# Two selective-scan layers on one core: D·u summed by TensorE, y gated straight out of PSUM, softplus sums and a Newton step on GpSimd, more scan inputs turned

## The chip, the cores and the metric

One Trainium2 chip, of which one core runs the whole program in one launch. The metric is the device time of one execution in microseconds; lower is better.

## What is computed

Four layers over x, float32, of shape (4, 128, 64, 64): a sparse 4096×4096 attention with a convolution (layer 0), a selective state-space scan with a depthwise convolution beside it (layer 1), a rank-one attention (layer 2), and a two-way selective scan with a group norm (layer 3). Only layers 1 and 3 are touched. Their core is the same:

```python
delta = softplus(dt @ W_dtr + b_dtr)                 # one rate per channel and step
h_l   = exp(delta_l * A) * h_(l-1) + delta_l * B_l * u_l   # N states per channel
y_l   = sum_n h_l[:, n] * C_l[n] + u_l * D
# layer 1: 128 channels, N = 64, one direction, 4 x 4096 steps; out = x + (y + conv) @ W_out
# layer 3: 256 channels, N = 16, 16384 steps forward, then 16384 backward;
#          out_dir = (y * silu(z)) @ W_out; the sum of both goes to the group norm
```

In layer 1, u is a layer-normed projection, so each step needs rsqrt(var), made from a root by logarithm and exponential and one Newton step.

## The kernel before, in words

Both scan layers work on 128 channels (partitions) and 1024 steps at a time. Layer 1 has 16 such **chunks** (index K), each with 64 states: 64 scans. Layer 3 has 64 **visits** (index S: 32 blocks of steps times two channel halves e, where K = S // 2; the first 32 visits run forward in time, the last 32 backward), each with 16 scans. States are handled in pairs P, k or r being the pair's number in its chunk (32 pairs) or visit (8 pairs). All order is written out by hand: each engine has its own list of steps, and semaphores join them. For every pair:

- ScalarE (ACT) writes the two decays exp(delta·A) of 128×1024 (`decays`, L884 and L1818). The second state of a pair, the odd one, has its channel halves swapped: it reads `crossed`, which two DMAs copy from `delta` once a chunk (`cross_delta`), after the last decay of the chunk before in layer 1.
- The input delta·B·u of the even state is made in one of two ways. *Broadcast*: TensorE (PE) spreads a row of B over 128 partitions into PSUM (`broadcast_B`, L702 and L1596) and VectorE (DVE) multiplies it by `du` in place (`even_input`, L1115 and L2005). *Turned*: ACT scales the transposed `duT` by B in eight 128×128 pieces (`turned_input`, L900; `odd_input` in layer 3, L1831) and PE transposes them back into PSUM (`turn_back`, L716 and L1606). The odd state's input is always turned; in layer 1, for the pairs in MADE, GpSimd (POOL) does the scaling instead, in one instruction (`odd_input`, L1025).
- DVE scans the two states (`scan`, L1128 and L2022), with the decay from SBUF and the input from PSUM. It may be at most four scans ahead of POOL's products (HS = 4), and ACT at most four decays ahead of DVE's scans (DS = 4).
- POOL multiplies h by the row C, which a DMA has broadcast into the same buffer (`product`, L1014 and L1943).
- PE adds the products up over the states in PSUM (`add_pair`, L733 and L1623), two pairs later. It uses the four 64×64 tiles of the array, own half to own half and own half to other half. Each float32 product appears as two instructions, so that a phase of `add_pair` is eight and a pair has two phases.

Once a chunk or visit comes the rest: projections and convolution on PE, softplus on ACT and POOL (`delta_copy`, `soft_exp`, `soft_log`, `soft_low`, `soft_max`, `soft_sum`, `input_rate`), u·D + y by DVE out of PSUM (`add_y`), then a POOL pass that adds the convolution (`add_conv`, L1008) or multiplies by the gate (`gating`, L1936). In layer 1 `rstds` and `newton` (L1069 to L1079) run on DVE at k = 7, and PE's `prep_rstd` and DVE's `scale_u` follow. In layer 3 `soft_max` (L1981) is on DVE at r = 3. PE keeps to its list: a step of it that waits holds up the `turn_back` and `broadcast_B` behind it, for which DVE's scans wait.

## Time and profile before

| | us |
|---|---|
| median of 3 runs (lowest, highest) | 10184.17 (10183.94, 10192.5) |
| profiled execution, its own time | 10189.69 |
| its span, first to last instruction | 10187.9 |
| busy in the span: PE, DVE, ACT, POOL | 9232.4, 8216.2, 7986.1, 5614.9 |
| layer 1: first scan to last scan | about 2840 to 5720 |
| layer 3: first scan to last scan | about 6784 to 10098 |

Layers 0 and 2 and the ends take the rest. An engine's busy share over the whole span mixes four layers and says little. What is needed is a table for stretches inside layer 1, the forward half of layer 3 and its backward half, divided by the number of chunks or visits that went by, which the number of scans gives. In a timeline row the columns are start, busy time, engine, line and operation, and the last bracket is the idle time before it and what ended that. Instructions overlap a little at their ends, so the price of one in a full queue is the distance between starts.

### The profile page before, as it was taken

The numbers are of one execution on the slowest core, as the hardware profiler recorded it, in microseconds if no ns is written. First come the engines' busy times: TensorE is split into PE (matmuls) and PEld (weight loads), VectorE is DVE, ScalarE is ACT, GpSimd is POOL, SyncE is SP. The second block draws the span as 40 slices with busy tenths as digits, with TensorE's granted clock in tenths as the row PEclk, the third lists the DMA queues.
The fourth block names the chain that finished last, engine by engine and source line by source line (L and its number), as shares of the span: only waits on it lengthen the run. The fifth ranks groups of instructions, "written<-read, shape, count | busy, mean of one in ns | idle before, by whom it ended". The sixth has DMA issues, their size and how long they took to land. (4 is left out here: it accounts for less than half of the span.)

```text
span 10187.9 us, 146443 instructions
## 1 busy us (share of the span) xinstructions
PE 9232.4 (91%) x51396; PEld 4770.3 (47%) x51396; DVE 8216.2 (81%) x6150; ACT 7986.1 (78%) x14637; POOL 5614.9 (55%) x2852
## 2 busy tenths in 40 slices
PE   9999999999988888888888999988899998888885
PEld 6767767767633333333433444433333333333332
DVE  7858858768589999999999511149999999999997
ACT  5646646646488999999999655569999999999995
POOL 0000000000089999999999300038888888888885
PEclk9999999999989999999999999999999999999997
DMA  0000000000055655555555200025555656556566
GB/s 39 0 1 0 0 1 0 0 0 0 3 170 190 191 189 186 196 191 193 188 193 196 84 8 8 8 91 193 195 199 193 199 195 201 192 194 201 193 197 225
DMA packets 338542, 1249.78 MB, mean 123 GB/s; under 512 B 39280, under 2 KB 39408, under 8 KB 334448
## 3 DMA queue, kind: packets, MB, share of 16 engines
q1 hardware_dynamic: 338032, 1243.13, 36.9%
q8 instruction: 301, 4.93, 0.2%
q14 instruction: 209, 1.71, 0.0%
HBM read 1144.41 MB, written 56.62 MB: 118 GB/s over the span
## 5 line engine op out<-in xcount | busy, mean ns | idle before, releaser
L1943 POOL TENSOR_TENSOR l_ring<-l_h,l_ring 128x1024 f32<-128x1024 f32 x1024 | 2095.1, 2058 | 517.7 <-DVE l_h L2022 516.3
L2022 DVE TENSOR_TENSOR_SCAN l_h<-l_ring,l_h,l_ps 128x1024 f32<-128x1024 f32 x960 | 2200.0, 2333 | 13.7 <-PE l_ps L1606 0.7
L1014 POOL TENSOR_TENSOR l_hc<-l_h,l_hc 128x1024 f32<-128x1024 f32 x1024 | 2027.9, 2000 | 165.4 <-DVE l_h L1128 144.2
L1128 DVE TENSOR_TENSOR_SCAN l_h<-l_decay,l_h,l_ps 128x1024 f32<-128x1024 f32 x768 | 1746.8, 2329 | 11.8 <-PE l_ps L716 5.0
L116 POOL COPY l_qm<-l_q 128x128 f32 x128 | 82.8, 648 | 2577.4 <-PE l_ps L188 2181.1
L900 ACT ACTIVATE l_xt<-l_duT,l_BT 128x128 f32<-128x128 f32 x4096 | 1247.3, 389 | 40.7 <-PE l_ps L716 40.2
L1831 ACT ACTIVATE l_xt<-l_duT,l_BT 128x128 f32<-128x128 f32 x4096 | 1246.8, 389 | 0.0
L1623 PE MATMUL l_ps<-l_ring,w_sb 64*64 64x512 f32 x8192 | 1170.1, 642 | 1.0 <-PE l_ps L1623 0.4
L733 PE MATMUL l_ps<-l_hc,w_sb 64*64 64x512 f32 x8192 | 1134.3, 624 | 0.6 <-PE l_ps L733 0.4
L212 PE MATMUL l_ps<-l_attnT,l_vT 128*128 128x128 f32 x8192 | 1096.5, 277 | 1.3 <-ACT l_attnT L283 1.3
L212 PEld LDWEIGHTS l_ps<-l_attnT,l_vT 128*128 128x128 f32 x8192 | 1014.8, 192 | 138.0 <-issue 114.7
L188 PE MATMUL l_ps<-l_k,l_qm 128*128 128x512 f32 x2048 | 1055.4, 600 | 16.7 <-DVE l_E L395 16.7
L716 PEld LDWEIGHTS l_ps<-w_sb,l_xt 128*128 128x128 f32 x5888 | 641.1, 142 | 878.2 <-DVE l_h L1128 714.0
L716 PE MATMUL l_ps<-w_sb,l_xt 128*128 128x128 f32 x5888 | 824.5, 283 | 231.0 <-DVE l_h L1128 154.9
L1255 PE MATMUL l_ps<-l_E,l_hs 128*128 128x512 f32 x2048 | 880.0, 592 | 5.2 <-DVE l_hs L1321 5.2
L401 DVE SCALAR_TENSOR_TENSOR l_E<-l_relu,l_E 128x1024 f32<-128x1024 f32 x512 | 626.6, 1224 | 287.3 <-ACT l_E L276 287.3
L276 ACT ACTIVATE l_E<-l_E,l_offsets 128x1024 f32<-128x1024 f32 x512 | 587.0, 1146 | 290.8 <-DVE l_E L395 290.7
L270 ACT ACTIVATE l_relu<-l_ps,l_offsets 128x1024 f32<-128x1024 f32 x512 | 570.8, 1115 | 273.6 <-PE l_ps L188 271.9
L1282 ACT ACTIVATE l_E<-l_g,l_neg_max,l_f 128x4096 f32<-128x4096 f32 x128 | 486.4, 3800 | 379.4 <-PE l_ps L1255 367.5
L1606 PEld LDWEIGHTS l_ps<-w_sb,l_xt 128*128 128x128 f32 x4096 | 477.5, 149 | 648.3 <-DVE l_h L2022 588.6
L1606 PE MATMUL l_ps<-w_sb,l_xt 128*128 128x128 f32 x4096 | 605.2, 295 | 172.6 <-DVE l_h L2022 170.4
L201 PEld LDWEIGHTS l_ps<-w_sb,l_E 128*128 128x128 f32 x4096 | 507.3, 141 | 410.2 <-issue 393.1
(238 smaller groups left out, 15173.8 us busy)
## 6 DMA issues: line engine op xcount, KB each, us to landing
l_hc<-l_rows_dram SPq DMA_DIRECT2D x1024, 512.0 KB, 4.7
l_ring<-l_rows_dram SPq DMA_DIRECT2D x1024, 512.0 KB, 4.9
l_crossed<-l_delta SPq DMA_DIRECT2D x160, 256.0 KB, 3.8
l_gate_dram<-l_gate SPq DMA_DIRECT2D x32, 512.0 KB, 6.6
l_recon_dram<-l_recon SPq DMA_DIRECT2D x32, 512.0 KB, 6.4
l_gate<-l_gate_dram SPq DMA_DIRECT2D x32, 512.0 KB, 5.5
l_xw<-x_dram SPq DMA_DIRECT2D x30, 513.5 KB, 6.2
x_dram<-x SPq DMA_DIRECT2D x16, 512.0 KB, 2.6
```

What stands on the lines that cost most here:

```text
L188: ins = nc.tensor.matmul(logits[c % 2][:, j * BANK:(j + 1) * BANK], qm[:, h, :], k[:, c * CH + j * BANK:c * CH + (j + 1) * BANK], start=Tr ...
L212: ins = nc.tensor.matmul(ps[:, bank, 0:128], vT[:, t * 128:(t + 1) * 128], attnT[:, g % 2, j * 128:(j + 1) * 128], start=t == 0, stop=t == ...
L716: ins = nc.tensor.transpose(state_bank(odd, hf)[:, t * 128:(t + 1) * 128], xt[:, (n + hf) % XS, t * 128:(t + 1) * 128], ident)
L733: ins = nc.tensor.matmul(ps[to, 4 + j, :], ident[own, own], hc[own, (2 * P + odd) % CS, half(j)], start=k == 0 and phase == 0, stop=k == P ...
L900: ins = nc.scalar.activation(into, own if odd else own[:, ::-1, :], ACT.Identity, scale=BT[:, p, blk, at:at + 1])
L1014: nc.gpsimd.tensor_tensor(hc[:, unit % CS, :], h[:, unit % HS, window(unit)][:, along(K)], hc[:, unit % CS, :], ALU.mult).then_inc(hc_done, 1)
L1128: nc.vector.tensor_tensor_scan(h[:, unit % HS, window(unit)][:, along(K)], decay[:, unit % DS, :], odd_in if odd else even_in, before, ALU ...
L1606: ins = nc.tensor.transpose(odd_bank(hf)[:, t * 128:(t + 1) * 128], xt[:, (2 * P + hf) % XS, t * 128:(t + 1) * 128], ident)
L1623: ins = nc.tensor.matmul(ps[to, 4 + j, :], ident[own, own], hc[own, (2 * P + odd) % CS, half(j)], start=r == 0 and phase == 0, stop=r == P ...
L1831: ins = nc.scalar.activation(xt[:, (2 * P + hf) % XS, t * 128:(t + 1) * 128], duT[:, S % 2, 4 * hf + t, :], ACT.Identity, scale=BT[:, K % ...
L1943: nc.gpsimd.tensor_tensor(hc[:, unit % CS, :], h[:, unit % HS, window(unit)][:, along], hc[:, unit % CS, :], ALU.mult).then_inc(hc_done, 1)
L2022: nc.vector.tensor_tensor_scan(h[:, unit % HS, window(unit)][:, into], decay[:, unit % DS, order], x_now[:, order], before, ALU.mult, ALU. ...
```

## The change

What it does, in both scan layers:

1. u·D is no longer computed by DVE. The weights hold D as a diagonal matrix, and PE adds D·u to the sum of states in PSUM, in the two own-half tiles, once a chunk or visit, in `add_pair` of pair 4.
2. DVE's one pass over the sum now adds the convolution (layer 1) or multiplies by the gate (layer 3) directly; POOL's passes `add_conv` and `gating` go. In layer 1 `gate_conv` moves from k = 1 to k = 0, ahead of it.
3. Softplus: ACT makes |z| and relu(z) from PSUM in halves; the full-width Abs, its drain and layer 1's full-width Relu go. In layer 3 `soft_max` becomes a plain addition on POOL.
4. Layer 1's Newton step moves to POOL (k = 7, ahead of the products); squares, variance and roots come one or two pairs earlier.
5. Layer 1 turns 16 even states a chunk instead of 14, and POOL makes 15 odd inputs instead of 14, in another pattern. Layer 3, which turned no even state and had POOL make none, now turns one a visit forward and two backward, and POOL makes two odd inputs a visit.
6. `delta` and `z1` start two elements further in; in layer 3 the rows of B and C sit at partitions 0 to 31 of `rest`, so POOL's `split_rest` waits for the turned B and for the stored rows.

The diff, cut to its core:

```diff
-TURNED = (1, 2, 3, 5, 7, 8, 9, 11, 15, 18, 25, 26, 29, 31)
-MADE = (0, 1, 3, 5, 8, 9, 13, 14, 15, 18, 19, 21, 29, 31)
+TURNED = (1, 2, 3, 5, 7, 9, 10, 11, 14, 18, 23, 25, 26, 28, 29, 31)
+MADE = (0, 1, 3, 5, 7, 10, 11, 13, 17, 19, 21, 23, 28, 29, 31)
...
+        delta = sb("delta", [128, 2, CH + 4])[:, :, 2:CH + 2]
+        z1, z2 = sb("z1", [128, CH + 4])[:, 2:CH + 2], sb("z2", [128, CH])
...
                 for own, other, j in ((lower, upper, phase), (upper, lower, 1 - phase)):
+                    if k == 4:
+                        nc.tensor.matmul(ps[own, 4 + j, :], wt("D")[own, own], u[own, P // PAIRS % 2, half(j)],
+                                         start=False, stop=False)
...
-                        if k in (2, 3):
-                            prep_u(K + 1, k - 2)
-                        if k == 7:
+                        if k in (1, 2):
+                            prep_u(K + 1, k - 1)
+                        if k == 5:
...
             def delta_copy(K, p, j):
                 act.wait_ge(delta_mm, 2 * K + j + 1)
-                nc.scalar.activation(delta[:, p, half(j)], prep_ps, ACT.Identity,
+                if j == 0:
+                    act.wait_ge(rows_stored, 16 * K + 16)
+                nc.scalar.activation(z1[:, half(j)], prep_ps, ACT.Abs, bias=wt("dtr_b"))
+                nc.scalar.activation(delta[:, p, half(j)], prep_ps, ACT.Relu,
                 act.wait_ge(delta_out, 2 * K + 2)
-                act.wait_ge(rows_stored, 16 * K + 16)
-                nc.scalar.activation(z1[:], delta[:, p, :], ACT.Abs)
-                act.drain()
                 nc.scalar.activation(z1[:], z1[:], ACT.Exp, scale=-1.0).then_inc(exp_ln, 1)
-                nc.scalar.activation(delta[:, p, :], delta[:, p, :], ACT.Relu)
...
-                        if k == 7:
+                        if k == 6:
...
+            def newton(K):
+                pool.wait_ge(root_ready, K + 1)
+                nc.gpsimd.tensor_tensor(tmp[:], var[:], root[:], ALU.mult)
+                pool.drain()
+                nc.gpsimd.tensor_tensor(tmp[:], tmp[:], root[:], ALU.mult)
+                pool.drain()
+                nc.gpsimd.tensor_scalar(tmp[:], tmp[:], -0.5, 1.5, ALU.mult, ALU.add)
+                pool.drain()
+                nc.gpsimd.tensor_tensor(rstd[:], root[:], tmp[:], ALU.mult).then_inc(var_rstd, 1)
...
-            def add_conv(K):
-                pool.wait_ge(g_out, 2 * K + 2)
-                pool.wait_ge(y_out, K + 1)
-                nc.gpsimd.tensor_tensor(yg[:], yg[:], cg[:], ALU.add).then_inc(yg_ready, 1)
...
+                    if K + 1 < NCH and k == 7:
+                        newton(K + 1)
...
-                    if k == 3 and K:
-                        add_conv(K - 1)
                     if K + 1 < NCH:
-                        if k == 4:
+                        if k == 3:
...
-            def add_y(K, p):
+            def add_y(K):
...
                 at_least(dve, out_mm, 2 * K)
-                nc.vector.scalar_tensor_tensor(out=yg[:], in0=u[:, p, :], scalar=wt("D"), in1=y_sum, op0=ALU.mult,
-                                               op1=ALU.add).then_inc(y_out, 1)
+                dve.wait_ge(g_out, 2 * K + 2)
+                nc.vector.tensor_tensor(yg[:], y_sum, cg[:], ALU.add).then_inc(yg_ready, 1)
...
-                    if k == 1 and K:
+                    if k == 0 and K:
...
                     if K + 1 < NCH:
-                        if k == 7:
+                        if k == 5:
                             rstds(K + 1)
-                            newton(K + 1)
...
-ODD_AT = DT_AT + R3
-C_AT = ODD_AT + S3 // 2
+ODD_AT = S3 // 2
+C_AT = S3
+TURNED3 = {True: (6,), False: (3, 6)}
+MADE3 = {True: (2, 6), False: (2, 6)}
...
+        delta = sb("delta", [128, 2, CH + 4])[:, :, 2:CH + 2]
+        BT = sb("BT", [128, 2, BLK, S3])
+        z1 = sb("z1", [128, CH + 4])[:, 2:CH + 2]
...
-                def turn_back(P):
+                def turn_back(P, odd):
+                    n = halves_before(P, odd)
+                    at_least(pe, scan_done, 2 * P + odd - 1)
+                    by_pool = odd and made(P)
+                    if by_pool:
+                        pe.wait_ge(xt_made, made_before[P] + 1)
                     for hf in range(2):
-                        pe.wait_ge(xt_ready, 2 * P + hf + 1)
+                        if not by_pool:
+                            pe.wait_ge(xt_ready, n + hf + 1 - 2 * made_before[P])
...
                         if r == 0:
-                            at_least(pe, y_out, S)
+                            at_least(pe, gated_ready, S)
...
                     for own, other, j in ((lower, upper, phase), (upper, lower, 1 - phase)):
+                        if r == 4:
+                            K, e = divmod(S, TI)
+                            at = L3_AT["D"].start + e * 128
+                            nc.tensor.matmul(ps[own, 4 + j, :], w[own, at + own.start:at + own.stop],
+                                             u[own, K % 2, e, half(j)], start=False, stop=False)
...
-                        broadcast_B(P + 1)
+                        if turned(P + 1):
+                            turn_back(P + 1, 0)
+                        else:
+                            broadcast_B(P + 1)
...
                 def delta_copy(T, j):
                     act.wait_ge(delta_mm, 2 * T + j + 1)
-                    nc.scalar.activation(delta[:, T % 2, half(j)], [V, U][j], ACT.Identity,
+                    if j == 0:
+                        at_least(act, delta_ready, T)
+                    nc.scalar.activation(z1[:, half(j)], [V, U][j], ACT.Abs, bias=col("dtr_b", T % TI))
+                    nc.scalar.activation(delta[:, T % 2, half(j)], [V, U][j], ACT.Relu,
...
                 def soft_exp(T):
-                    at_least(act, delta_ready, T)
-                    nc.scalar.activation(z1[:], delta[:, T % 2, :], ACT.Abs)
-                    act.drain()
...
-                    at_least(act, low_ready, T)
-                    at_least(act, delta_ready, T)
...
+                            ins = nc.scalar.activation(into, own if odd else own[:, ::-1, :], ACT.Identity,
+                                                       scale=BT[:, K % 2, blk, at:at + 1])
...
                     if P + 1 < NS * PAIRS:
+                        if turned(P + 1):
+                            turned_input(P + 1, 0)
                         decays(2 * P + 2)
-                        odd_input(P + 1)
+                        if not made(P + 1):
+                            turned_input(P + 1, 1)
...
                 def split_rest(K):
                     pool.wait_ge(part_ready, 2 * K + 1)
+                    pool.wait_ge(bt_mm, K + 1)
+                    pool.wait_ge(rows_stored, 16 * K + 16)
...
+                def soft_max(T):
+                    pool.wait_ge(exp_ln, 3 * T + 3)
+                    nc.gpsimd.tensor_tensor(delta[:, T % 2, :], delta[:, T % 2, :], z2[:], ALU.add).then_inc(max_ready, 1)
...
-                def gating(S):
-                    K, e = divmod(S, TI)
...
-                    nc.gpsimd.tensor_tensor(yg[:, S % 3, :], yg[:, S % 3, :], gate[:, e, :], ALU.mult).then_inc(gated_ready, 1)
+                def odd_input(P):
+                    pool.wait_ge(duT_out, 2 * S + 2)
+                    pool.wait_ge(bt_ready, K + 1)
+                    n = halves_before(P, 1)
+                    at_least(pool, xt_mm, n + 2 - XS)
+                    into = xt[:, n % XS:n % XS + 2, :].rearrange("p s (t d) -> p (s t) d", d=128)
+                    at = S3 // 2 + r
+                    nc.gpsimd.tensor_tensor(into, duT[:, S % 2, :, :],
+                                            BT[:, K % 2, :, at:at + 1].broadcast_to([128, BLK, 128]),
+                                            ALU.mult).then_inc(xt_made, 1)
...
+                    if P + 1 < NS * PAIRS and made(P + 1):
+                        odd_input(P + 1)
-                    if r == 2 and S:
-                        gating(S - 1)
...
-                def soft_max(T):
-                    dve.wait_ge(exp_ln, 3 * T + 3)
-                    own = delta[:, T % 2, :]
-                    nc.vector.scalar_tensor_tensor(out=own, in0=own, scalar=0.0, in1=z2[:], op0=ALU.max,
-                                                   op1=ALU.add).then_inc(max_ready, 1)
...
+                def gating(S):
...
                         dve.wait_ge(out_mm, 2 * ((S - 3) // TI) + 2)
-                    nc.vector.scalar_tensor_tensor(out=yg[:, S % 3, :], in0=u[:, K % 2, e, :], scalar=col("D", e),
-                                                   in1=y_sum, op0=ALU.mult, op1=ALU.add).then_inc(y_out, 1)
+                    if forward(K):
+                        dve.wait_ge(gate_out, 2 * S + 2)
+                    else:
+                        dve.wait_ge(gate_loaded, 16 * (S - NCH * TI) + 16)
+                    nc.vector.tensor_tensor(yg[:, S % 3, :], y_sum, gate[:, e, :], ALU.mult).then_inc(gated_ready, 1)
...
-                    if S + 1 < NS:
-                        if r == 3:
-                            soft_max(S + 1)
...
-                        add_y(S - 1)
-                    if P + 1 < NS * PAIRS:
+                        gating(S - 1)
+                    if P + 1 < NS * PAIRS and not turned(P + 1):
...
+               ("beta", 0, column(beta)), ("dtr_b", 0, column(b_dtr)), ("D", 0, _np.diag(D_param))]
+                    ("dtr_b", e, column(bdt[own])), ("D", e * 128, _np.diag(D[own]))]
```

## Rows read from the trace of the kernel before

**Rows 1.** Stretches: us; busy (count) PE, PEld, DVE, ACT, POOL; clock; DMA; GB/s

```profile
3000.00:5700.00 2700.00, 2368.51 (x15356) 1049.87 (x15348) 2645.78 (x1418) 2452.96 (x5202) 2532.39 (x1284) 0.98 0.58 192
6850.00:8460.00 1610.00, 1447.16 (x7891) 567.68 (x7890) 1568.78 (x835) 1592.67 (x3145) 1383.56 (x661) 0.97 0.60 196
8460.00:10090.00 1630.00, 1397.53 (x7662) 548.91 (x7660) 1584.95 (x882) 1493.17 (x2937) 1361.90 (x651) 0.94 0.60 196
```

**Rows 2.** The same stretches, the scans alone: DVE busy (count)

```profile
3000.00:5700.00 2700.00, 2184.09 (x961) 0.98 0.58 192
...
6850.00:8460.00 1610.00, 1152.26 (x503) 0.97 0.60 196
8460.00:10090.00 1630.00, 1141.48 (x499) 0.94 0.60 196
```

**Rows 3.** Timeline of DVE, a Newton step in layer 1

```profile
3782.70 0.14 DVE L1069 TENSOR_SCALAR l_var<-l_ps 128x8 f32<-128x8 f32 x1
3784.03 1.78 DVE L1073 TENSOR_TENSOR l_tmp<-l_var,l_root 128x8 f32<-128x8 f32 x1 [1.19 <-ACT l_root L811]
...
3789.71 0.17 DVE L1079 TENSOR_TENSOR l_rstd<-l_root,l_tmp 128x8 f32<-128x8 f32 x1
```

**Rows 4.** Timeline of DVE in layer 3, a pair and soft_max

```profile
7419.00 1.21 DVE L2005 TENSOR_TENSOR l_ps<-l_du,l_ps 128x1024 f32<-128x1024 f32 x1
7420.24 4.58 DVE L2022 TENSOR_TENSOR_SCAN l_h<-l_ring,l_h,l_ps 128x1024 f32<-128x1024 f32 x2
7424.75 1.21 DVE L2005 TENSOR_TENSOR l_ps<-l_du,l_ps 128x1024 f32<-128x1024 f32 x1
7425.86 3.06 DVE L1981 SCALAR_TENSOR_TENSOR l_delta<-l_delta,l_z 128x1024 f32<-128x1024 f32 x1
```

**Rows 5.** Durations, ns min/median/max, then first and last start: soft_max; product

```profile
L1981 DVE SCALAR_TENSOR_TENSOR l_delta<-l_delta,l_z x64: 1219/3055/3077, 6771.9 to 10025.1; 128x1024 f32<-128x1024 f32 x64
...
L1943 POOL TENSOR_TENSOR l_ring<-l_h,l_ring x1024: 1984/1998/3005, 6786.1 to 10098.7; 128x1024 f32<-128x1024 f32 x171
```

**Rows 6.** Timeline of ACT in layer 1: half copy, turned input, softplus

```profile
3837.82 0.67 ACT L846 ACTIVATE l_delta<-l_ps,w_sb 128x512 f32<-128x512 f32 x1
3838.39 2.43 ACT L900 ACTIVATE l_xt<-l_duT,l_BT 128x128 f32<-128x128 f32 x8
3840.73 1.13 ACT L884 ACTIVATE l_decay<-l_delta,w_sb 128x1024 f32<-128x1024 f32 x1
...
3845.46 1.04 ACT L852 ACTIVATE l_z<-l_delta 128x1024 f32<-128x1024 f32 x1
3846.57 1.06 ACT L854 ACTIVATE l_z<-l_z 128x1024 f32<-128x1024 f32 x1
3847.54 1.04 ACT L855 ACTIVATE l_delta<-l_delta 128x1024 f32<-128x1024 f32 x1
```

**Rows 7.** Costliest groups on POOL: count, busy, mean ns, idle before

```profile
L1025 POOL TENSOR_TENSOR l_xt<-l_duT,l_BT 128x1024 f32<-128x1024 f32 x224 | 429.2, 1916 | 17.2 <-PE l_ps L716 13.4 <-issue 3.7
...
L1936 POOL TENSOR_TENSOR l_yg<-l_yg,l_gate 128x1024 f32<-128x1024 f32 x64 | 151.4, 2366 | 4.8 <-DVE l_yg L1989 4.8
...
L116 POOL COPY l_qm<-l_q 128x128 f32 x128 | 82.8, 648 | 2577.4 <-PE l_ps L188 2181.1 <-ACT l_q L254 396.2
```

**Rows 8.** Timeline of PE in layer 3

```profile
7409.21 1.09 PE L1623 MATMUL l_ps<-l_ring,w_sb 64*64 64x512 f32 x8
7410.23 0.60 PE L1596 MATMUL l_ps<-l_stack,sel 96*128 96x512 bf16 x2
...
7413.14 1.88 PE L1545 MATMUL l_ps<-l_xw,l_taps 128*128 128x512 f32 x4
...
7440.46 1.09 PE L1606 MATMUL l_ps<-w_sb,l_xt 128*128 128x128 f32 x8
```

**Rows 9.** Timeline at a chunk boundary of layer 1: ACT, then DVE

```profile
3919.86 1.15 ACT L884 ACTIVATE l_decay<-l_crossed,w_sb 128x1024 f32<-128x1024 f32 x1 [5.15 <-DMA l_crossed<-l_delta]
...
3934.24 1.28 DVE L1102 SCALAR_TENSOR_TENSOR l_yg<-l_u,w_sb,l_ps 128x1024 f32<-128x1024 f32 x1 [3.83 <-PE l_ps L733]
```

107 lines of the change are left out of this document (46 added, 61 removed).

## The prediction

> **What bounds the kernel now.** First the busy table of three stretches, divided by the work that went by in them [rows 1, 2]. In 3000 to 5700 us 961 scans ran, 15.0 chunks of layer 1: 179.8 us a chunk. In the forward half of layer 3 503 scans in 1610 us are 31.4 visits of 51.2 us; in the backward half 499 in 1630 us are 31.2 visits of 52.3 us. Busy time per chunk or visit, by the same division:
>
> | | PE | DVE | ACT | POOL | period |
> |---|---|---|---|---|---|
> | layer 1, chunk | 157.7 | 176.2 | 163.3 | 168.6 | 179.8 |
> | layer 3, forward | 46.0 | 49.9 | 50.7 | 44.0 | 51.2 |
> | layer 3, backward | 44.8 | 50.8 | 47.9 | 43.7 | 52.3 |
>
> In layer 1 and backward DVE has the least left over. Forward it is ACT, with DVE 0.8 us behind it. That difference decides what the change can be worth: everything taken from DVE beyond the next engine's load is lost.
>
> Then DVE's timeline, to see what of its busy time is work. The Newton step's instructions have 8 columns. One takes 0.17 us, but the first of them 1.78 [rows 3], and from the end of `rstds` to the end of `newton` 7.0 us pass (3782.84 to 3789.88), 1.2 of them a wait for ACT's root. Layer 3's `soft_max` takes 3.06 us at the median and 1.22 at best [rows 5]. The best of the products on POOL is 1.98 us and the worst 3.0. So these two DVE steps, which alone here read both operands from SBUF while POOL is at work, are stretched by POOL and stretch it. The page "SBUF — State Buffer" of the Trainium skill (section "SBUF: two separate sides") says why: DVE instructions with two SBUF inputs and GpSimd's take one port pair in turns, for a whole instruction each. The trace agrees, by the rows just named.
>
> **Layer 1, part by part, per chunk.** *DVE.* Newton gone: −7.0. Two more turned even states: an even input costs 1.24 from its start to the scan's (7419.00 to 7420.24) [rows 4], −2.5. `add_y` stays one pass over PSUM with one operand fewer; the nearest such pass is the even input of 1.21, so I count it at nothing, and moving `gate_conv` ahead of it too. D·u on PE therefore frees POOL of a pass, not DVE. Sum −9.5: a chunk whose order stays DVE's takes 170.3.
>
> *ACT.* One more state is turned on it (33 instead of 32: two even more, one odd fewer): eight pieces cost 2.34 (3838.39 to 3840.73). Abs with its drain −1.11 (3845.46 to 3846.57), full Relu −0.97 (by its neighbour's spacing), two half-width Abs from PSUM +0.57 each (3837.82 to 3838.39) [rows 6]. Net +1.4, so 164.7. But at the chunk boundary ACT waits for `crossed`, 5.15 us in the chunk shown, and DVE then waits 3.8 for the sum behind it [rows 9]. That wait stays, because the two DMAs still follow the last decay: ACT needs some 170 of 170.3.
>
> *POOL.* One odd input more +1.92, `add_conv` gone −2.37 (the same kind of pass as `gating`) [rows 7]. The four small Newton instructions lie between nothing and four of the 128×128 copy of 0.65, 2.6 in all; being 8 columns wide they are nearer the low end, with three drains, and I take 1.5. The two-element shift of `delta` and `z1` touches four softplus passes of 2.4 us. Products, which read h at shifted starts, take 2.0 [rows 5]; so the gain is between nothing and 4 × 0.37 = 1.5, and I take half, 0.7. Net +0.3: 168.9. The Newton step waits on POOL in front of the products of pair 7, and the sums behind those on PE; ACT is up to four decays ahead, so the root should be there.
>
> *PE.* Two `turn_back` for two broadcasts, (1.09 − 0.60) × 2 = 1.0, and D·u, below; it has 20 us free.
>
> Three engines within 2 us of each other and at most two pairs of slack between them will not run at 170.3. Before, DVE lost 3.6 us a chunk with 8 us of room to POOL. I add 2.7 for the hand-overs: 173.0, a gain of 6.8 × 16 = **109 us**. Bounds 170.3 (152 us) and 176.5 (53 us).
>
> **Layer 3, per visit.** *DVE.* `soft_max` −3.0; one even input forward, two backward, −1.24 each; `add_y` to `gating` nothing. Forward 49.9 − 4.2 = 45.7, backward 50.8 − 5.5 = 45.3.
>
> *ACT.* Odd inputs 8 before. Forward two go to POOL and one even state comes: −2.34. Backward two go, two come: 0. Softplus +0.03 (1.11 against two halves). So 48.4 forward and 47.9 backward.
>
> *POOL.* Two odd inputs +3.8, `soft_max` +2.2, `gating` −2.4, less the stretch of the products by `soft_max`, about −1.0 (from 2.0 to 3.0 once a visit) [rows 5, 7]: 46.6 and 46.3. The new waits of `split_rest` hold the products behind it; turning B is one pair earlier on PE, so nothing is charged.
>
> *PE.* Turned states +0.5 and +1.0. D·u is the unknown. A phase of `add_pair` is eight 64×512 instructions and takes 1.02 (7409.21 to 7410.23), while four 512-column instructions on the full array take 1.88, 0.47 each [rows 8]: so four tiles run at once, two instructions each. With D·u each own-half tile has four to do instead of two. If the tiles run independently the phase is two instructions longer, 0.94, and a visit 1.9. If the loads of the other tiles queue behind a busy one, the two own-half tiles are passed one after the other, twice that, 3.8. I take 1.9, since the present phase already shows no queueing. PE then has 48.4 forward and 47.7 backward. (The page "TensorEngine Tiling (Array Packing)" of the Trainium skill, "Key Properties", has tiles load and multiply in parallel; by it the sum is the one with 1.9, by queueing the one with 3.8, which is a rival below.)
>
> So forward ACT and PE are level at 48.4, backward at 47.9 and 47.7, all above DVE. Before, the busiest engine idled 0.5 and 1.5 us a visit. With two engines level I add 0.8 forward and 1.1 backward: 49.2 and 49.0. Gain 2.0 × 32 = **64** and 3.3 × 32 = **106 us**.
>
> Sum 109 + 64 + 106 = 279, from the execution's own 10189.7 (its span is 10187.9): 9911. The median of the runs is 5.5 lower: **9905 us**.
>
> **Rivals.** (a) *PE becomes layer 3's bound.* With 3.8 for D·u PE has 50.3 and 49.6; with 0.5 and 0.8 on top the periods are 50.8 and 50.4. Gain 0.4 × 32 + 1.9 × 32 = 74, with layer 1's 109: 183, so 10001. For it: PE works in order and is the busiest after the change. Against: the 1.02 of a phase.
>
> (b) *The engines fit closely.* Layer 1 at 170.3 and layer 3 at 48.6 and 48.3, close to the busiest engine as the forward half is now (50.7 in 51.2): 152 + 83 + 128 = 363, so 9821. For it: ACT forward has a margin of 0.5 only. Against: no stretch shows three engines level.
>
> (c) *DVE stays the bound and all that it loses is gained:* 152 + 4.2 × 32 + 5.5 × 32 = 462, so 9722. Against: ACT's 48.4 and 47.9.
>
> (d) *Slower: D·u breaks the four-tile overlap.* Were all twelve instructions of the phase serial at 0.47, it would take 5.6 instead of 1.0, and a visit 9.2 more: PE 55.7 and 55.0, a loss of 4.5 and 2.7 a visit, 230 us against layer 1's 109: 10305. It decides from about 7.3 us a visit for D·u, where PE (46.5 and 45.8 without it) costs layer 3 the 109 us. Against: nothing like it is seen in this tile shape now.
>
> (e) *The change does little:* layer 1's hand-overs eat its gain (176.5 or more) and (a) holds: 53 + 74 = 127 or less, 10060.
>
> **Numbers.** Forecast 0.38, (a) 0.22, (b) 0.2, (c) 0.03, (d) 0.05, (e) 0.12. The forecast's own range is 9865 to 9955; from 9810 to 10045 all but (c), (d) and part of (e) lie inside. Two tenths of a per cent, 20 us, is what a measurement here can tell from no change. Faster 0.91, within it 0.03 (the tail of (e)), slower 0.06.
>
> **What would show it.** Chunks of 173 and visits of 49.2 and 49.0 us. No DVE instruction with 8 columns over 0.2 us, and no product over 2.1. DVE busy near 169, 45.7 and 45.3. The phase of pair 4 on PE about 2.0 us: 3 speaks for (a), 5 or more for (d). ACT's idle time almost gone in layer 3's forward half, and DVE's idle time now ended by PE (`turn_back`, `broadcast_B`). The forecast is wrong if PE stalls at its own k = 5 or k = 8 for squares or the root on POOL, or if POOL's product rate turns out to bind layer 1.

## The result, and the profile after

The median of 20 runs is 10105.49 us (10092.8 to 10199.81), that of 20 runs of the kernel before 10184.12 (10175.27 to 10199.26). The ratio is 0.9927 (95% interval 0.9916 to 0.9938): 79 us gained where 279 were forecast, and the time lies above the range. The profiled execution took 10118.55 us.

The busy table of three stretches, its columns as in [rows 1], and then the same stretches with the scans alone, as in [rows 2]:

```profile
3000.00:5600.00 2600.00, 2323.06 (x15014) 1042.41 (x15010) 2423.45 (x1275) 2377.38 (x5100) 2410.88 (x1289) 0.96 0.59 190
6850.00:8440.00 1590.00, 1491.25 (x8300) 616.58 (x8292) 1438.41 (x767) 1513.47 (x2912) 1410.72 (x719) 0.97 0.61 197
8440.00:10030.00 1590.00, 1433.36 (x8364) 602.11 (x8363) 1447.09 (x797) 1499.34 (x2991) 1413.26 (x720) 0.98 0.64 202
...
3000.00:5600.00 2600.00, 2090.74 (x918) 0.96 0.59 190
6850.00:8440.00 1590.00, 1145.80 (x500) 0.97 0.61 197
8440.00:10030.00 1590.00, 1151.67 (x504) 0.98 0.64 202
```

Divided as before the change (918 scans are 14.3 chunks; 500 and 504 are 31.25 and 31.5 visits), with the forecast in brackets:

| | PE | DVE | ACT | POOL | period |
|---|---|---|---|---|---|
| layer 1, chunk | 162.0 | 169.0 (169) | 165.7 (164.7) | 168.1 (168.9) | 181.3 (173.0) |
| layer 3, forward | 47.7 (48.4) | 46.0 (45.7) | 48.4 (48.4) | 45.1 (46.6) | 50.9 (49.2) |
| layer 3, backward | 45.5 (47.7) | 45.9 (45.3) | 47.6 (47.9) | 44.9 (46.3) | 50.5 (49.0) |

The work came out close to what was added up: DVE, ACT and layer 1's POOL within 1.0, and PE and POOL in layer 3 below their estimates. The periods did not. Layer 1 has 12 us a chunk in which even its busiest engine does nothing, layer 3 some 2.5 to 3 a visit. So the loss isn't work but waiting, and the waits have to be read.

The list of waits names them; a row is waiting line and engine, what ended the wait, us in total, times, longest. First the kernel before, 3000 to 5700 us, then the kernel after, 3000 to 5600, then after in layer 3, 6850 to 9700:

```profile
DVE l_h L1128 <- PE l_ps L716: 5.0, 7, 0.8
```

```profile
DVE l_h L1124 <- PE l_ps L717: 115.6, 36, 7.8
...
PE l_ps L601 <- ACT l_u L807: 74.8, 14, 5.4
...
DVE l_ps L2036 <- PE l_ps L1605: 103.3, 111, 2.6
...
PE l_ps L1619 <- POOL l_xt L1967: 90.9, 43, 2.7
DVE l_h L2053 <- PE l_ps L1619: 90.6, 55, 2.3
```

In layer 1 DVE's scan waits for `turn_back` on PE 115.6 us, 8.1 a chunk; the chunk is 8.3 longer than forecast. PE in turn waits once a chunk (14 times) for ACT's `u_copy` in line 601, which is `prep_u`. In layer 3 DVE waits for PE in both ways (for the broadcast and for the turned state) 193.9 us, 3.5 a visit, where the kernel before has 19.3 in the same window, and PE waits for POOL's odd input.

**Layer 1: what stands in the queue.** The timeline of PE around one such wait, then ACT's, then DVE's:

```profile
3924.28 1.02 PE L601 MATMUL l_ps<-x,w_sb 128*128 128x512 f32 x2
...
3931.41 0.66 PE L717 MATMUL l_ps<-w_sb,l_xt 128*128 128x128 f32 x4 [0.45 <-ACT l_xt L901]
3937.44 2.05 PE L601 MATMUL l_ps<-x,w_sb 128*128 128x512 f32 x2 [5.37 <-ACT l_u L807]
3939.41 1.99 PE L737 MATMUL l_ps<-l_hc,w_sb 64*64 64x512 f32 x8
3941.33 1.97 PE L717 MATMUL l_ps<-w_sb,l_xt 128*128 128x128 f32 x8
```

```profile
3916.65 1.15 ACT L885 ACTIVATE l_decay<-l_crossed,w_sb 128x1024 f32<-128x1024 f32 x1 [5.58 <-DMA l_crossed<-l_delta]
...
3932.30 2.43 ACT L901 ACTIVATE l_xt<-l_duT,l_BT 128x128 f32<-128x128 f32 x8
...
3936.72 0.57 ACT L807 ACTIVATE l_u<-l_ps 128x512 f32<-128x512 f32 x1
```

```profile
3930.92 4.58 DVE L1124 TENSOR_TENSOR_SCAN l_h<-l_decay,l_h,l_ps 128x1024 f32<-128x1024 f32 x2
3943.34 4.58 DVE L1124 TENSOR_TENSOR_SCAN l_h<-l_decay,l_h,l_ps 128x1024 f32<-128x1024 f32 x2 [7.84 <-PE l_ps L717]
```

The change puts `prep_u` at PE's k = 1 and 2 instead of 2 and 3. Its second half writes into the bank of the first, so it waits until ACT has copied that out (`u_copy`, at ACT's k = 2, which was not moved). ACT works its own queue in order. It has just waited 5.58 us for `crossed` at the chunk boundary and still has turned inputs and the decays of pair 3 ahead of the copy. PE works in order too, so `add_pair` and the `turn_back` that DVE needs stand behind a preparation for the next chunk that nobody wants yet. PE idles 5.37 us, DVE 7.84: its pause begins 3.4 us after PE's, but it ends 5.9 us later. In these 5.9 us PE works at half speed. The three groups after its pause take 2.05, 1.99 and 1.97 us, where the first `prep_u` took 1.02 and an `add_pair` phase and a `turn_back` take 1.09. That is some 2.8 us of DVE's 7.84. The stretches around it, columns as in [rows 1], show the granted clock at 1.00 (2.4 GHz) ahead of the idle time and at 0.50, the lower of its two levels (1.2 GHz), after it:

```profile
3925.00:3931.00 6.00, 4.28 (x29) 1.67 (x28) 5.72 (x5) 5.99 (x18) 5.58 (x4) 1.00 0.26 105
3937.00:3943.00 6.00, 5.56 (x18) 2.37 (x18) 0.00 (x0) 1.85 (x4) 0.98 (x1) 0.50 0.01 3
```

**Layer 3: a late input in front of the long phases.** POOL, PE and DVE in one visit, timelines:

```profile
7416.99 2.00 POOL L1940 TENSOR_TENSOR l_z<-l_z 128x1024 f32<-128x1024 f32 x1
7418.95 2.01 POOL L1944 TENSOR_TENSOR l_delta<-l_delta,l_z 128x1024 f32<-128x1024 f32 x1
...
7430.69 2.00 POOL L1955 TENSOR_TENSOR l_du<-l_delta,l_u 128x1024 f32<-128x1024 f32 x1
7432.66 1.91 POOL L1967 TENSOR_TENSOR l_xt<-l_duT,l_BT 128x1024 f32<-128x1024 f32 x1
```

```profile
7431.65 1.09 PE L1641 MATMUL l_ps<-l_ring,w_sb 64*64 64x512 f32 x8
7434.72 1.46 PE L1619 MATMUL l_ps<-w_sb,l_xt 128*128 128x128 f32 x8 [1.97 <-POOL l_xt L1967]
7435.97 1.91 PE L1588 MATMUL l_ps<-w_sb,l_du 128*128 128x128 f32 x8
7437.81 1.04 PE L1638 MATMUL l_ps<-l_u,w_sb 64*64 64x512 f32 x1
...
7440.08 0.61 PE L1605 MATMUL l_ps<-l_stack,sel 96*128 96x512 bf16 x2
7440.62 0.64 PE L1638 MATMUL l_ps<-l_u,w_sb 64*64 64x512 f32 x1
...
7442.50 1.09 PE L1619 MATMUL l_ps<-w_sb,l_xt 128*128 128x128 f32 x8
```

```profile
7436.21 2.35 DVE L2053 TENSOR_TENSOR_SCAN l_h<-l_ring,l_h,l_ps 128x1024 f32<-128x1024 f32 x1 [1.85 <-PE l_ps L1619]
7440.73 1.23 DVE L2036 TENSOR_TENSOR l_ps<-l_du,l_ps 128x1024 f32<-128x1024 f32 x1 [2.16 <-PE l_ps L1605]
```

POOL has four softplus passes of 2.0 us between its products at that place, and the odd input of pair 6 behind the last. PE, which is through with the phase ahead at 7432.7, waits 1.97 for it. Then follow on PE the two phases with D·u: the sums of pair 4 are added two pairs later, at r = 6. The first takes 2.27 (7437.81 to 7440.08), the second 1.88 (7440.62 to 7442.50), where a phase took 1.02 [rows 8]. The broadcast between them comes that much later. DVE loses 1.85 and 2.16 us, 4 us in this visit.

Here too the pause costs clock. The granted clock was 1.00 from 7425 to 7431, and after PE's idle time it is at the lower level, as in layer 1, though for a shorter time. The first two groups behind the pause in the run e5 below, behind a wait of 0.68 instead of 1.97, are at full speed. The changed kernel's stretch, then e5's timeline:

```profile
7436.00:7437.80 1.80, 1.80 (x9) 1.48 (x7) 1.59 (x1) 1.76 (x3) 1.80 (x2) 0.50 0.90 332
```

```profile
7438.99 1.06 PE L1619 MATMUL l_ps<-w_sb,l_xt 128*128 128x128 f32 x8 [0.68 <-POOL l_xt L1967]
7439.89 1.04 PE L1588 MATMUL l_ps<-w_sb,l_du 128*128 128x128 f32 x8
```

Their 1.46 and 1.91 us in the changed kernel, and the 2.27 instead of 1.88 of the first long phase, are 1.6 us of half clock. It is mostly a matter of the forward half, where the mean granted clock is 0.97 here (6850 to 8440 us) and 1.00 in e2 and e5 (6850 to 8300).

**Where the time of the layers is.** From the first scan's start to the last's in each profiled execution, the sum over a layer needs no choice of a window. The rows are the kernel after's, by source line: durations ns min/median/max, first and last start. Then the same of the kernel before:

```profile
L1124 DVE TENSOR_TENSOR_SCAN l_h<-l_decay,l_h,l_ps x768: 2315/2322/2349, 3012.6 to 5722.1; 128x1024 f32<-128x1024 f32 x192
L1124 DVE TENSOR_TENSOR_SCAN l_h<-l_decay,l_zero,l_ps x256: 2316/2322/2349, 2836.6 to 5188.0; 128x1024 f32<-128x1024 f32 x128
...
L2053 DVE TENSOR_TENSOR_SCAN l_h<-l_ring,l_h,l_ps x960: 2318/2326/2351, 6889.6 to 10031.5; 128x1024 f32<-128x1024 f32 x192
L2053 DVE TENSOR_TENSOR_SCAN l_h<-l_ring,l_zero,l_ps x64: 2320/2341/2350, 6787.9 to 8515.3; 128x1024 f32<-128x1024 f32 x64
```

```profile
L1128 DVE TENSOR_TENSOR_SCAN l_h<-l_decay,l_h,l_ps x768: 2314/2322/2350, 3016.5 to 5712.5; 128x1024 f32<-128x1024 f32 x192
L1128 DVE TENSOR_TENSOR_SCAN l_h<-l_decay,l_zero,l_ps x256: 2316/2322/2349, 2840.0 to 5182.1; 128x1024 f32<-128x1024 f32 x128
...
L2022 DVE TENSOR_TENSOR_SCAN l_h<-l_ring,l_h,l_ps x960: 2311/2329/2350, 6888.3 to 10095.9; 128x1024 f32<-128x1024 f32 x192
L2022 DVE TENSOR_TENSOR_SCAN l_h<-l_ring,l_zero,l_ps x64: 2314/2333/2349, 6783.6 to 8524.7; 128x1024 f32<-128x1024 f32 x64
```

Layer 1 went from 2872.5 to 2885.5 us: 13.0 lost where 109 were to be gained. Layer 3 went from 3312.3 to 3243.6: 68.7 gained of 170. Start, middle and tail gave 15.4 that nobody had forecast. Together 71.1, the difference of the two profiled executions (10189.69 and 10118.55).

### The profile page after: what moved, and what is told of

Its sections match the earlier page's. It is cut to its first block and busy times, and to the rows that moved or that the text cites. A ratio compares the mean times of both kernels' runs of the same rounds, so it can differ in the third digit from the quotient of the medians.

```text
span 10116.8 us, 149065 instructions
## 1 busy us (share of the span) xinstructions
PE 9352.1 (92%) x52804; PEld 4901.3 (48%) x52804; DVE 7820.4 (77%) x5894; ACT 7933.1 (78%) x14573; POOL 5667.6 (56%) x3044
## 5 line engine op out<-in xcount | busy, mean ns | idle before, releaser
L1976 POOL TENSOR_TENSOR l_ring<-l_h,l_ring 128x1024 f32<-128x1024 f32 x1024 | 2028.6, 1997 | 371.7 <-DVE l_h L2053 371.4
L901 ACT ACTIVATE l_xt<-l_duT,l_BT 128x128 f32<-128x128 f32 x4224 | 1287.0, 389 | 89.8 <-PE l_ps L717 87.9
L1641 PE MATMUL l_ps<-l_ring,w_sb 64*64 64x512 f32 x8192 | 1242.2, 620 | 1.2 <-ACT l_gate L1776 0.5
L1852 ACT ACTIVATE l_xt<-l_duT,l_BT 128x128 f32<-128x128 f32 x3840 | 1170.7, 391 | 24.1 <-PE l_ps L1619 22.7
L737 PE MATMUL l_ps<-l_hc,w_sb 64*64 64x512 f32 x8192 | 1175.6, 631 | 1.0 <-POOL l_hc L1020 0.6
L717 PEld LDWEIGHTS l_ps<-w_sb,l_xt 128*128 128x128 f32 x6144 | 672.6, 143 | 850.9 <-DVE l_h L1124 643.2
L717 PE MATMUL l_ps<-w_sb,l_xt 128*128 128x128 f32 x6144 | 860.4, 283 | 179.0 <-DVE l_h L1124 88.1
L1619 PE MATMUL l_ps<-w_sb,l_xt 128*128 128x128 f32 x4864 | 693.1, 286 | 241.1 <-DVE l_h L2053 110.9
L1619 PEld LDWEIGHTS l_ps<-w_sb,l_xt 128*128 128x128 f32 x4864 | 539.2, 144 | 764.3 <-DVE l_h L2053 529.6
```

The source lines that it names most:

```text
L717: ins = nc.tensor.transpose(state_bank(odd, hf)[:, t * 128:(t + 1) * 128], xt[:, (n + hf) % XS, t * 128:(t + 1) * 128], ident)
L737: ins = nc.tensor.matmul(ps[to, 4 + j, :], ident[own, own], hc[own, (2 * P + odd) % CS, half(j)], start=k == 0 and phase == 0, stop=k == P ...
L901: ins = nc.scalar.activation(into, own if odd else own[:, ::-1, :], ACT.Identity, scale=BT[:, p, blk, at:at + 1])
L1619: ins = nc.tensor.transpose(state_bank(odd, hf)[:, t * 128:(t + 1) * 128], xt[:, (n + hf) % XS, t * 128:(t + 1) * 128], ident)
L1641: ins = nc.tensor.matmul(ps[to, 4 + j, :], ident[own, own], hc[own, (2 * P + odd) % CS, half(j)], start=r == 0 and phase == 0, stop=r == P ...
L1852: ins = nc.scalar.activation(into, own if odd else own[:, ::-1, :], ACT.Identity, scale=BT[:, K % 2, blk, at:at + 1])
```

## The experiments

All were timed beside runs of the kernel before, whose median was 10189.49, 10189.83 and 10186.43 us in the three batches; ratios are to it. The last two columns are the spans from first to last scan, worked out as above and divided by 16 chunks and 64 visits (before 179.5 and 51.8, after 180.3 and 50.7). In layer 1 they lie up to 1 us below the periods of the stretches, by which the forecast was made.

| kernel | median us | ratio (95% interval) | chunk | visit |
|---|---|---|---|---|
| e1: prep_u at k = 2, 3 | 9975.36 | 0.9794 (0.9777 to 0.9810) | 171.1 | 50.7 |
| e1b: prep_u at k = 1, 3 | 9980.74 | 0.9798 (0.9782 to 0.9814) | 171.3 | 50.7 |
| e2: POOL's inputs at pairs 2, 7 | 10018.76 | 0.9837 (0.9820 to 0.9853) | 178.8 | 49.4 |
| e3: without D·u | 9987.14 | 0.9804 (0.9788 to 0.9820) | 179.2 | 48.9 |
| e4: e1 and e2 | 9901.54 | 0.9717 (0.9701 to 0.9733) | 171.8 | 49.5 |
| e5: layer 3's D·u in pair 1 | 9964.23 | 0.9778 (0.9762 to 0.9794) | 179.1 | 48.5 |
| e6: e4, Newton on DVE | 9932.58 | 0.9750 (0.9734 to 0.9767) | 173.3 | 49.5 |
| e7: e4, soft_max on DVE | 9905.90 | 0.9725 (0.9708 to 0.9741) | 171.4 | 49.6 |
| e8: e4, no shift | 9972.69 | 0.9790 (0.9774 to 0.9806) | 172.8 | 50.4 |
| e9: e1 and e5 | 9844.65 | 0.9665 (0.9649 to 0.9681) | 172.0 | 48.6 |
| e10: e9 and e2 | 9853.93 | 0.9675 (0.9658 to 0.9691) | 171.8 | 48.8 |
| e11: e4, layer 1's old tables | 9931.14 | 0.9750 (0.9734 to 0.9766) | 173.5 | 49.5 |

### Layer 1: prep_u back where it was (e1), and its second half alone (e1b)

```diff
-                        if k in (1, 2):
-                            prep_u(K + 1, k - 1)
+                        if k in (2, 3):
+                            prep_u(K + 1, k - 2)
```

> The changed kernel with one step put back in layer 1: TensorE's prep_u(K+1) at k = 2 and 3, as before, instead of k = 1 and 2. Layer 3 is untouched. Theory A (order on TensorE): in the changed kernel the second prep_u stands at k = 2 and waits for ScalarE's u_copy, which ScalarE has at its own k = 2, behind inputs for the next pair; TensorE's transposes queue behind it and VectorE loses 7.8 us once a chunk. Then the chunk falls from 181.3 us to about 173.5, the 7.8 us idle before a scan is gone, and the time falls by 8 x 15 = about 120 us, to some 9985 us. Theory B (three engines too close, and ScalarE's wait for the crossed rates at the chunk boundary): the lost time only moves to another wait at the boundary, the chunk stays over 179 and the time within 30 us of the changed kernel's.

130 us came back between the medians (142 between the profiled executions; layer 1's own span is 148 shorter, 2885.5 to 2737.8). In the list of waits of 3000 to 5400 us PE's wait for `u_copy` is gone, and DVE's wait for `turn_back` is 6.5 us in all instead of 115.6. ACT's wait for `crossed`, which theory B blames, is still there (49.1 us, 14 times), and the time came back all the same:

```profile
DVE l_h L1124 <- PE l_ps L717: 6.5, 17, 0.6
```

The chunk, 171.4 by the stretch (896 scans in 2400 us, 14.0 chunks), is below the 173.0 forecast. PE's granted clock in the stretch is 1.00 instead of 0.96, and its busy time 158.1 a chunk (2213.79 us) instead of 162.0. The work is the same, so the 3.9 us are laid to the half clock, 2.8 of them to the three groups above. e1b moves only the second half:

```diff
-                        if k in (1, 2):
-                            prep_u(K + 1, k - 1)
+                        if k in (1, 3):
+                            prep_u(K + 1, k // 2)
```

> The changed kernel with only the second prep_u of layer 1 moved, from k = 2 to k = 3; the first stays at k = 1. Theory A: the waiting step is the second one alone, so this gains as much as moving both or slightly more (about 120 us, chunk about 173), since ScalarE's first u_copy then never waits for TensorE. Theory B: no gain over 30 us.

It agrees with e1 within 6 us. The first half at k = 1 costs nothing that the runs can tell; the wait of the second for ACT is the whole cause.

### Layer 3: POOL's late input (e2), no D·u at all (e3), D·u elsewhere (e5)

```diff
-MADE3 = {True: (2, 6), False: (2, 6)}
+MADE3 = {True: (2, 7), False: (2, 7)}
```

> The changed kernel with one table entry of layer 3 changed: GpSimd makes the odd inputs of pairs 2 and 7 of a visit instead of 2 and 6. Layer 1 is untouched. Theory A (GpSimd late at r = 5): in the changed kernel the input of pair 6 is made behind four softplus passes of 2.0 us, TensorE waits for it some 2 us, its queue stands and VectorE loses 2 to 4 us a visit. Then visits fall from 50.9 and 50.5 us to 49.5 or less, and the time by 64 x 1.0 to 64 x 1.5 = 65 to 95 us. Theory B (the extra matmuls of D*u make TensorE the bound, rival a of the prediction): the visit stays within 0.4 us, the time within 25 us. Theory C: the wait moves to pair 7 as GpSimd is just as late there; no gain either, but with TensorE's wait for l_xt still of the same size.

87 us. With pair 7's odd input made by POOL instead of pair 6's, PE's wait for POOL's input is 4.0 us in the window of 6850 to 9700, where it was 90.9, and the visit is 49.4 instead of 50.7. PE's busy time in the forward half falls from 47.7 to 46.9 a visit with the same work, since the half clock is gone there too. How the gain divides between the queue and the clock no run tells: the edit takes away both.

e3 takes out both of these matmuls, of layer 1 and of layer 3:

```diff
-                    if k == 4:
-                        nc.tensor.matmul(ps[own, 4 + j, :], wt("D")[own, own], u[own, P // PAIRS % 2, half(j)],
-                                         start=False, stop=False)
...
-                        if r == 4:
-                            K, e = divmod(S, TI)
-                            at = L3_AT["D"].start + e * 128
-                            nc.tensor.matmul(ps[own, 4 + j, :], w[own, at + own.start:at + own.stop],
-                                             u[own, K % 2, e, half(j)], start=False, stop=False)
```

> The changed kernel without the D*u matmuls in both scan layers: u*D is left out of y. It prices them. Rival a (TensorE bound in layer 3): visits fall by the 1.9 us that the two longer phases take, 64 x 1.9 = 120 us. Theory A (the loss in layer 3 is the wait for GpSimd's odd input at pair 6, just ahead of these phases): they lie behind a stall and partly beside other waits, so a visit falls by 0.3 to 1 us, 20 to 65 us in all. Layer 1's chunk changes by less than 1 us in both.

118 us, what rival (a) had for it (120). The visit fell by 1.8, forward more than backward (2.4 and 1.2 by the stretches). PE's busy time falls by nearly as much (2.4 and 1.0; 45.3 and 44.5 are left), so the work was paid in full, although PE was idle 3.2 us a visit forward. The two phases are 1.7 us longer with D·u at full clock; the rest of these differences goes with the granted clock, which rises from 0.97 to 0.99 forward and falls from 0.98 to 0.97 backward. My theory, which had most of it hidden, was too low. The waits of 6850 to 9700 us in e3:

```profile
PE l_ps L1616 <- POOL l_xt L1959: 91.7, 50, 2.7
DVE l_h L2045 <- PE l_ps L1616: 84.4, 67, 3.0
...
DVE l_ps L2028 <- PE l_ps L1602: 20.4, 14, 2.1
```

DVE's wait for the broadcast fell from 103.3 to 20.4 us, while the waits for POOL's input and for the turned state stayed (91.7 and 84.4, after 90.9 and 90.6). So the matmuls are paid in front of the broadcast, and the late input by itself. Does PE's time as such bind, or only this place? e5 tells that:

```diff
-                        if r == 4:
+                        if r == 1:
```

> The changed kernel (GpSimd still makes the input of pair 6) with D*u of layer 3 added at pair 1 instead of pair 4, so that its two longer phases run on TensorE at r = 3 and not at r = 6, behind the wait for GpSimd. Without D*u a visit was 2.4 us shorter forward and 1.1 backward. If its cost comes from standing in the late pair, the visits fall to 49.6 to 50.2 us and the time by 30 to 65 us. If the work itself costs what it takes (TensorE is the bound), nothing changes within 15 us. It can also lose: the step at r = 3 has a four-instruction convolution piece, so a new stall there would make it slower than the changed kernel.

141 us, more than twice what I expected, with the same instructions. The visit is 48.5, even shorter than without D·u at all. So the matmuls cost nothing that shows in another pair, and what they cost in pair 4 is their place: directly behind the late input and, forward, in the half clock that its pause leaves. The waits of 6850 to 9700 us in e5 show that PE still waits for POOL (57.7 us), but DVE's two waits for PE fell from 193.9 to 92.7:

```profile
DVE l_ps L2036 <- PE l_ps L1605: 59.9, 87, 1.0
...
PE l_ps L1619 <- POOL l_xt L1967: 57.7, 57, 1.5
...
DVE l_h L2053 <- PE l_ps L1619: 32.8, 49, 1.3
```

Why e5's visit is 0.4 shorter than e3's isn't settled. By the stretches the difference is nearly all in the backward half (48.7 against 49.3 us; forward 48.3 and 48.4), where the granted clock is 0.99 in e5 and 0.97 in e3. PE's wait for POOL is shorter in e5 (57.7 against 91.7), which fits a PE that has its extra work ahead of that wait instead of behind it, but no run was made to show that.

### Both mended (e4), and the best version (e9, e10)

e4 has the edits of e1 and of e2.

> The changed kernel with both edits: prep_u(K+1) at k = 2 and 3 on TensorE in layer 1, and GpSimd's odd inputs at pairs 2 and 7 in layer 3. If the two stalls are separate and are what the prediction missed, the gains add: 130 us from the one and 87 from the other below the changed kernel, some 9890 us, with chunks of 171.3 and visits of 49.2 and 49.6 us as in the two runs apart. That would lie within 15 us of the forecast of 9905. If the layers share the cause (a slower state of the clock, say), the sum is less.

9901.54 us: 12 us short of the two gains added, and within 4 us of the forecast of 9905. That closeness is luck in part, and no proof of each term. By the stretches a chunk takes 172.0 against the 173.0 forecast and a visit 49.3 and 49.6 against 49.2 and 49.0. In all, layer 1 gives 124 us for the 109 forecast, layer 3 144 for 170, and start, middle and tail, which were not forecast, 17: the misses cancel. e9 has the edits of e1 and e5, and e10 those of e2 beside them:

> The changed kernel with prep_u late in layer 1 and D*u added at pair 1 in layer 3, GpSimd still at pairs 2 and 6. The two gains seen apart were 130 and 141 us below the changed kernel. If they add: some 9835 us, chunks of 171.3, visits of 48.4 and 48.6 us. If the place of D*u only mattered because layer 1 shifted nothing, it is the same; a sum short by over 25 us would say that one of the gains was of the chip and not of the order.

> As the run with D*u at pair 1, and GpSimd's odd inputs at pairs 2 and 7 too. If the stall at pair 6 has two causes in a row (late input, then the long phases), then with the long phases gone the late input still costs TensorE some 0.4 us a visit, and moving it gains 0 to 25 us more. If ScalarE, with 48.3 of 48.4 us forward, is now the bound there, nothing is left to gain forward, and the move of an odd input onto it at pair 6 can cost a little.

e9 is the fastest, 9844.65 us, 10 us short of the sum of its two gains, 3.35% below the kernel before and 261 us below the changed one. Its forward stretch (6850 to 8200 us) shows ACT busy in 1345.54 of 1350 us; there is next to nothing left to win there by order alone.

e10 is 9 us slower than e9, inside the intervals. PE still waits 59.8 us for POOL in e9 (6850 to 9700 us), but with D·u out of the way POOL's late input costs nothing measurable. Of the two repairs of layer 3, moving D·u gives more (48.6 us a visit in e9, 49.5 in e4), and the other adds nothing to it.

### What the moved work itself is worth: Newton (e6), soft_max (e7), shift (e8), tables (e11)

These start from e4, so that the two stalls don't cover them. e6 has the four instructions of `newton` on DVE again, at k = 7 behind `rstds` at k = 5:

```diff
-                    if K + 1 < NCH and k == 7:
-                        newton(K + 1)
...
+                        if k == 7:
+                            newton(K + 1)
```

> The kernel with both edits, and layer 1's Newton step back on VectorE at k = 7. Step of the prediction: it costs VectorE 7.0 us a chunk, stretched by GpSimd's use of the shared port. If VectorE is the bound again and the stretch returns, its 8-column instructions take 1.6 to 1.9 us each and a chunk grows from 171.3 to about 177 or 178, 95 to 110 us. If GpSimd was the tighter engine, the chunk grows by under 2 us.

31 us, a third of what I expected, and 1.6 us a chunk by the span. DVE's busy time rises by 1.9 a chunk (2356.92 us for 883 scans, 2356.68 for 893 in e4), where the prediction had 7.0 for the step. The first and the second instruction by source line in e6 (durations ns min/median/max, first and last start), then the second in the kernel before:

```profile
L1066 DVE TENSOR_TENSOR l_tmp<-l_var,l_root x16: 161/1532/1825, 2788.7 to 5313.3; 128x8 f32<-128x8 f32 x16
...
L1068 DVE TENSOR_TENSOR l_tmp<-l_tmp,l_root x16: 166/168/169, 2788.9 to 5314.7; 128x8 f32<-128x8 f32 x16
```

```profile
L1075 DVE TENSOR_TENSOR l_tmp<-l_tmp,l_root x16: 167/1882/1887, 2792.1 to 5410.1; 128x8 f32<-128x8 f32 x16
```

Before, three of the four were stretched to 1.8 or 1.9 us; in e6 only one is, the others take 0.17, and the wait of 1.2 for the root is gone too, since the root is there before `newton` comes. So of the 7.0 us the earlier root and the undisturbed instructions give 5, and taking the step off DVE 2. The trace shows what leaves them undisturbed: a pause of POOL. Before, POOL ran without a gap through the step (3778.01 to 3789.61 in the chunk of [rows 3]). In e6's chunk of 3226 us, `newton`'s first instruction runs from 3226.48 to 3228.07; POOL's product ends at 3228.04 and POOL then waits 3.15 us for DVE's next scan, while the other three pass from 3228.14 on, 0.17 us each. The new table gives POOL no odd input at that place (pair 8), where the old one did; that this opens the pause is read from the code and not tested by itself.

e7 has `soft_max` on DVE at r = 3, as the plain addition:

```diff
+                    if S + 1 < NS and r == 3:
+                        soft_max(S + 1)
```

> The kernel with both edits, and layer 3's soft_max back on VectorE at r = 3 (as a plain addition). Step of the prediction: VectorE has 46.0 us of work in a visit of 49.2 to 49.6, so its first 3 us are free. The instruction takes 3.0 us as before. If only sums count, a visit grows by 0 to 0.5 us, 0 to 30 us in all. If order counts as much as it did in the two stalls, it stands between two scans and a visit grows by 1 to 3 us, 60 to 190 us.

4 us, nothing. DVE then has 48.0 us a visit forward, still below ACT. The addition takes 2.24 us at the median there, where the one with max took 3.06 (`delta` also starts two elements further in), and the longest of POOL's products is 3.004 again, as before [rows 5], where the kernel after has 2.013.

e8 takes the two elements away:

```diff
-        delta = sb("delta", [128, 2, CH + 4])[:, :, 2:CH + 2]
+        delta = sb("delta", [128, 2, CH])
-        z1, z2 = sb("z1", [128, CH + 4])[:, 2:CH + 2], sb("z2", [128, CH])
+        z1, z2 = sb("z1", [128, CH]), sb("z2", [128, CH])
...
-        z1 = sb("z1", [128, CH + 4])[:, 2:CH + 2]
+        z1 = sb("z1", [128, CH])
```

> The kernel with both edits (late prep_u, GpSimd's inputs at pairs 2 and 7), without the two-element shift of delta and z1. Step of the prediction: the shift saves GpSimd up to 0.37 us in each of four softplus passes. In the trace after, they take 2.00 us instead of 2.37. If the shift is the cause they go back to 2.37, GpSimd has 1.5 us more to do per chunk and visit; in layer 1, where it is within 4 us of the period, the chunk grows by 0.5 to 1.5 us, and the time by 10 to 60 us. If the shift is not the cause they stay at 2.00 and nothing changes.

71 us, above what I expected. One pass by its source line, first with the shift (the kernel after), then without it (e8):

```profile
L1940 POOL TENSOR_TENSOR l_z<-l_z x64: 1992/2000/2008, 6776.8 to 9956.9; 128x1024 f32<-128x1024 f32 x64
```

```profile
L1940 POOL TENSOR_TENSOR l_z<-l_z x64: 2351/2365/2383, 6657.1 to 9827.1; 128x1024 f32<-128x1024 f32 x64
```

The other three change alike (2.365 to 2.374 on average without the shift, 2.00 with it), so it is 0.365 us on each of four passes, the upper bound of the prediction's term (1.5), not half of it. In layer 3 the visit changes by 0.9 (49.5 to 50.4), though POOL isn't the busiest engine there: its passes stand ahead of the next input in its queue, so their length becomes PE's wait. In 6850 to 9700 us PE waits 45.8 us for POOL's odd input in e8 (29 times, up to 1.9), where e4 has 4.5, and DVE waits 44.9 us for `turn_back` instead of 17.8.

e11 has the old tables of layer 1, with 14 turned even states and 14 inputs by POOL:

```diff
-TURNED = (1, 2, 3, 5, 7, 9, 10, 11, 14, 18, 23, 25, 26, 28, 29, 31)
-MADE = (0, 1, 3, 5, 7, 10, 11, 13, 17, 19, 21, 23, 28, 29, 31)
+TURNED = (1, 2, 3, 5, 7, 8, 9, 11, 15, 18, 25, 26, 29, 31)
+MADE = (0, 1, 3, 5, 8, 9, 13, 14, 15, 18, 19, 21, 29, 31)
```

> The kernel with both edits, with the tables of layer 1 as they were before the change (14 turned even states and 14 inputs by GpSimd instead of 16 and 15). Step of the prediction: two more turned states take 2.5 us from VectorE in a chunk whose order is VectorE's. Then the chunk grows from 171.8 to some 174.3, 35 to 45 us. If the pattern was what let the engines fit (GpSimd and ScalarE being level with VectorE), it grows by more, over 60 us; if VectorE is not the bound, by less than 15.

30 us, 1.7 a chunk, under the 2.5 that two even inputs less on DVE are worth and a little under the 35 to 45 us expected.

## Why the prediction was wrong

**What held.** The way of summing: all nine loads of DVE, ACT and POOL came out within 1.5 us. No product is longer than 2.035 us in layer 1 and 2.013 in layer 3 (3.005 before [rows 5]), so `soft_max` on DVE no longer holds POOL up, and with it back on DVE the 3.0 returns (e7). The phase with D·u takes 1.88 us, close to the 1.96 from which the forecast came; rival (d), 5.6, is refuted, and (a) too, as PE has 47.7 and 45.5 of work, not 50.3 and 49.6. (The page "TensorEngine Tiling (Array Packing)" of the Trainium skill, "Key Properties", has the tiles work in parallel; the trace agrees with 12 instructions in 1.88 us, where one after the other at 0.47 they would take 5.6.) And e4, with the same work and two steps placed elsewhere, has the time forecast, though by misses that cancel. (The sum for layer 1's DVE mixes two things: 170.3 is the old period less 9.5, not a load. By its load, 176.2, and the 8.3 of the 9.5 that were busy time, it would be 167.9; the text forecasts 169 and 169.0 was measured.)

**Where it failed, layer 1.** The step is "it has 20 us free" for PE, with "I add 2.7 for the hand-overs: 173.0" behind it. The diff moves `prep_u`, and the prediction costs neither its move nor its wait. That PE had 20 us free says nothing of when. The one wait takes 8.1 us of DVE's time a chunk, and without it layer 1 is 148 us shorter (e1). The rows had the warning: ACT's wait of 5.15 for `crossed` at the chunk boundary [rows 9], which the prediction read as ACT's own problem. An engine that comes 5 us late to k = 0 is late for everybody who waits for its k = 2. The last paragraph of the prediction names stalls at PE's k = 5 or 8; it was the right kind of fault at the wrong step.

**Where it failed, layer 3.** The step is "I add 0.8 forward and 1.1 backward", all that the sum has for waiting. "Two odd inputs +3.8" counts POOL's new inputs as work only, and no term asks when they come. Measured are 2.5 and 2.9 above the busiest engine. POOL's input of pair 6 is queued behind four softplus passes, PE waits for it, and the two phases with D·u come right after it. e2 (87 us) takes the wait away and e5 (141 us) the long phases; with e5's edit the other adds nothing (e10). The prediction added D·u as work of 1.9 us a visit and never asked which `broadcast_B` or `turn_back` stands behind it, and when DVE wants that.

**Sizes.** The 7.0 us a chunk for the Newton step stand in the sum rightly, but not by the move to POOL, which e6 puts at 1.9 (31 us / 16). The shift was put at 0.7 in layer 1 and left out of layer 3's sum for POOL; it is 1.5 in both (e8), and POOL's load in layer 3 came out 1.5 and 1.4 below the estimate. `soft_max` on POOL gives nothing (e7), as the prediction's own rule says: what DVE loses below ACT's load is lost. Start, middle and tail gave 15 us that were not in the sum.

**The rivals.** In time the result lies beyond (e), 10060, but it isn't (e): there the hand-overs of layer 1 cost 6.2 us a chunk and PE binds layer 3. Here layer 1 lost everything, through one wait. Layer 3's periods, 50.9 and 50.5, are those of rival (a), 50.8 and 50.4, but by coincidence: (a) had them from 3.8 us of D·u on PE, and PE has 3.2 and 5.0 us a visit to spare.

## What to carry to other kernels

When a diff moves a step of an in-order engine, list what that step waits for and where the engine that ends this wait is in its own queue at that time; then list what stands behind it. A step that is idle work for later (here the next chunk's projection) must never stand in front of one that the bound engine needs now. A sum of busy times gives a lower bound that an order can reach: here two edits of a line or two each were worth 204 us (e4) or 261 (e9) on nearly the same instructions.

Extra work on an engine with room costs nothing or a little more than its length (2.1 us a visit between the changed kernel and e5, for 1.7 us of work), depending on whether it follows a late operand. Put it away from such a wait, and try two places before judging it.
